# A two-layer cross-attention kernel: writes and loads of the stacked Q and K, their order on a queue, and two helpers' work moved between engines

## What is computed

```python
h = jnp.concatenate([x, latents], axis=1)             # 64 + 512 keys
q = (latents @ q_w + q_b).reshape(b, k_len, NH, DH)   # 512 queries
kv = (h @ kv_w + kv_b).reshape(b, p + k_len, NH, DH, 2)
attn = jnp.einsum('bkhd,bnhd->bhkn', q, kmat) / DH
attn = jax.nn.softmax(jnp.where(full_mask[:, None, None, :], attn, -jnp.inf), axis=-1)
attn_out = jnp.einsum('bhkn,bnhd->bkhd', attn, v).reshape(b, k_len, H)
attn_out = attn_out @ out_w + out_b + residual
out = gelu(rmsnorm(attn_out, postnorm_w) @ mlp_w1 + mlp_b1) @ mlp_w2 + mlp_b2
return out + residual
```

## Time and profile before

| | |
|---|---|
| median of three runs | 1864.66 us (1859.7 to 1866.77) |
| profiled execution, its own time | 1862.46 us |
| its span, first to last instruction | 1860.6 us |
| TensorE busy | 1642.2 us, 88% |
| VectorE busy | 1009.4 us, 54% |
| ScalarE busy | 703.4 us, 38% |
| GpSimd busy | 541.9 us, 29% |
| mean granted TensorE clock | 0.93 of 2.4 GHz |
| second attention, first scores to last | 766 to 1432 us |

### The profile page before, as it was taken

One profiled execution on the slowest core, in us unless ns is written; L12 is line 12 of the kernel. 1 busy time (PEld: TensorE's weight loads), 2 busy tenths in 40 slices (PEclk: granted clock), 3 DMA queues, 4 the chain that ended last, 5 costly groups with the idle time before them and its releaser, 6 DMA issues.

```text
span 1860.6 us, 23089 instructions
## 1 busy us (share of the span) xinstructions
PE 1642.2 (88%) x6993; PEld 1229.6 (66%) x6993; DVE 1009.4 (54%) x1612; ACT 703.4 (38%) x1260; POOL 541.9 (29%) x543
## 2 busy tenths in 40 slices
PE   5778887899999998888988898989886699999998
PEld 4667775667878786555665555655553477787886
DVE  3665565554333335667766766775787455334333
ACT  3433333431111111367556745663667232111111
POOL 2232245404040505133323422341358210404000
PEclk9788898999999998789988999998988799999999
DMA  5011023501010215223123223221221420101011
GB/s 176 1 40 63 23 91 100 177 1 46 0 45 0 91 70 186 68 83 112 61 72 94 87 61 109 65 91 61 95 84 46 151 81 1 46 0 45 0 41 50
DMA packets 60730, 126.13 MB, mean 68 GB/s; under 512 B 10397, under 2 KB 10722, under 8 KB 60642
## 3 DMA queue, kind: packets, MB, share of 16 engines
q1 hardware_dynamic: 53602, 102.08, 16.8%
q0 software_dynamic: 7040, 23.07, 4.1%
HBM read 90.25 MB, written 34.60 MB: 67 GB/s over the span
## 4 chain that ended last, share of the span: by engine, by line
PE 70%; DVE 14%; issue 6%; ACT 4%; DMA 3%; SPq 1%; POOL 0%; ACTq 0%; DVEq 0%; POOLq 0%
PE bank L2064 18%; PE bank L2052 17%; PE bank L1926 5%; DVE RA L1268 4%; PE bank L1961 3%; PE bank L1922 3%; PE bank L2023 3%; DVE FA L1501 3%; PE bank L1976 3%; PE bank L1977 2%; PE bank L1939 2%; PE bank L1748 2%; PE bank L1724 2%; PE bank L1943 2%; PE bank L1799 1%
## 5 line engine op out<-in xcount | busy, mean ns | idle before, releaser
L2064 PE MATMUL bank<-W,RA 128*128 128x512 f32 x1536 | 384.3, 402 | 25.3 <-DVE RA L1268 25.1
L2052 PE MATMUL bank<-RA,W 128*128 (+1 forms) x1536 | 374.7, 396 | 2.7 <-issue 2.3
L2064 PEld LDWEIGHTS bank<-W,RA 128*128 128x128 f32 x1536 | 290.3, 191 | 99.5 <-DVE RA L1268 31.2
L841 POOL TENSOR_TENSOR RA<-FA,RA 128x512 fp32r<-128x512 f32 (+1 forms) x160 | 216.0, 1354 | 423.9 <-ACT FA L1104 423.8
L2052 PEld LDWEIGHTS bank<-RA,W 128*128 128x128 f32 x1536 | 286.9, 188 | 74.9 <-issue 5.9
L1268 DVE TENSOR_TENSOR RA<-FA,RA 128x512 fp32r<-128x512 f32 (+2 forms) x308 | 274.7, 894 | 68.0 <-ACT FA L1104 54.5
L1160 ACT ACTIVATE FA<-bank,cols 128x512 f32<-128x512 f32 x128 | 88.2, 689 | 560.2 <-PE bank L2052 560.1
L1631 DVE CAST RA<-FA 128x512 fp32r<-128x512 f32 x128 | 62.5, 488 | 368.9 <-ACT FA L1160 368.7
L1103 ACT ACTIVATE RA<-bank 128x512 fp32r<-128x512 f32 (+1 forms) x320 | 192.4, 601 | 170.3 <-PE bank L1961 164.6
L1501 DVE TENSOR_REDUCE FA<-bank 128x1 f32<-128x512 f32 x256 | 169.1, 685 | 65.4 <-PE bank L1939 64.1
L1104 ACT ACTIVATE FA<-bank 128x512 f32<-128x512 f32 (+1 forms) x320 | 191.5, 599 | 0.0
(11 more groups left out here) (149 smaller groups left out, 1838.1 us busy)
## 6 DMA issues: line engine op xcount, KB each, us to landing
RA<-k_parts SPq DMA_DIRECT2D x96, 144.0 KB
FA<-after_layer SPq DMA_DIRECT2D x12, 1024.0 KB, 6.2
RA<-q_parts SPq DMA_DIRECT2D x96, 128.0 KB
k_parts<-FA SPq DMA_DIRECT2D x16, 576.0 KB, 3.2
after_att<-FA SPq DMA_DIRECT2D x32, 256.0 KB, 2.1
q_parts<-FA SPq DMA_DIRECT2D x16, 512.0 KB, 2.7
raw<-in_L_xattn_mlp_w_dram POOLq DMA_DIRECT2D x32, 256.0 KB, 3.4
RA<-after_att SPq DMA_DIRECT2D x12, 512.0 KB, 8.6
```

The costliest lines, as they stand in the source:

```text
L841: pool.tensor_tensor(pl[0:m, r, :], pf[0:m, r, :], ph[0:m, r, :].bitcast(F32), ALU.subtract).then_inc(p_lo_pool, 1)
L2052: op = pe.matmul(bank[FC1_BANK[i]][:, :], W[:, slot, a, k, i * P:(i + 1) * P], yT_[:, ds(b * (2 * KT * S) + (d * KT + k) * S, S)], start=( ...
L2064: op = pe.matmul(bank[4 + t][:, :], gs[:, a, i, t * P:(t + 1) * P], W[:, slot + 1, d, i, :], start=(i == 0 and a == 0 and d == 0), stop=(i ...
```

## The change

It does five things, all in the second attention.

1. `q_parts` and `k_parts` in DRAM hold, for each head, the three blocks of 32 rows in stacking order, one of them twice. `parts` issues three writes of [128 rows, 512 or 576] where there was one of [128, 2, 512 or 576].
2. `stack` loads 96 rows in one DMA for Q and one for K, where it took three each. Counts of the semaphores follow.
3. On SyncE's queue `pair(0)` stands behind `max_row`, and `pair(1)` behind sum row 2.
4. `lo_by_pool`: GpSimd makes the low parts of all four full tiles of a head and VectorE that of the context tile; before, GpSimd had two full tiles and every second context tile.
5. The copy of a head's result to `sg` is VectorE's, ahead of its sum in `o_sum`; ScalarE's `o_out` goes.

```diff
-    return t in (1, 3) or (t == TT and j % 2 == 0)
+    return t < TT
...
-STACK = 16 * 13
+STACK = 16 * 5
 def stack_count(c):
-    return 16 * 7 if c < 2 else STACK
+    return 16 * 3 if c < 2 else STACK
...
 def parts(x, nb, c):
...
-    sp.dma_start((q_parts, k_parts)[x][c % 2], (qt, kt)[x].bitcast(F32)).then_inc(parted[x][c % 2], 16)
+    to = (q_parts, k_parts)[x][c % 2]
+    for r, part in enumerate(((0, 0, 1), (0, 1, 0))[x]):
+        sp.dma_start(to[:, r, :, :], (qt, kt)[x][:, part, :].bitcast(F32)).then_inc(parted[x][c % 2], 16)
 def stack(nb, c, half):
...
-    for x, dst_, src_, order_ in ((0, QS, q_parts, (0, 0, 1)), (1, KS, k_parts, (0, 1, 0))):
-        wait_apart(sp, (parted[x][c % 2], at(0, nb, 32, 16 * (c // 2 + 1))))
-        rows_of = src_[c % 2].rearrange("(j p) h n -> p j h n", p=HD)
-        for r, part in enumerate(order_):
-            sp.dma_start(dst_[r * HD:(r + 1) * HD, c % 2, heads, :].bitcast(F32),
-                         rows_of[:, heads, part, :]).then_inc(to, 16)
+    for x, dst_, src_ in ((0, QS, q_parts), (1, KS, k_parts)):
+        wait_apart(sp, (parted[x][c % 2], at(0, nb, 96, 48 * (c // 2 + 1))))
+        sp.dma_start(dst_[0:3 * HD, c % 2, heads, :].bitcast(F32),
+                     src_[c % 2, heads].rearrange("j r p n -> (r p) j n")).then_inc(to, 16)
...
     if ahead:
         wait_apart(sp, (pb_free, at(0, b, USES, use1(f"{pre}KC{nc_}", last) + 1)))
         parts(1, nb, nc_)
-        pair(0)
     sums(HG * c + 1)
     if not (last and c == G - 1):
...
         max_row(b if c + 1 < G else b + 1, (c + 1) % G)
     if ahead:
+        pair(0)
+    sums(HG * c + 2)
+    if ahead:
         pair(1)
-    sums(HG * c + 2)
...
 def o_sum(h):
     j = h % HG
+    dve.wait_ge(pv_step, at(0, b, BSTEP, (h + 1) * (TT + 1)))
+    wait_apart(dve, (o_moved[h % 2], at(0, b, 128, 16 * (h // 2))))
+    dve.tensor_copy(sg[0:2 * HD + 1, h % 2, :], bank[6 + h % 2][0:2 * HD + 1, :]).then_inc(sg_ready, 1)
     dve.wait_ge(sg_ready, at(0, b, H, h + 1))
...
-parts = [nc.dram_tensor(n, (2, P, 2, m), F32, kind="Internal").ap() ...
+parts = [nc.dram_tensor(n, (2, HG, 3, HD, m), F32, kind="Internal").ap() ...
```

More of the change, by code:

```diff
@@ L335, in program @@
         pv_step = sem("pv_step")
+        o_free = sem("o_free")
         sg_ready = sem("sg_ready")
-        o_free = sem("o_free")
         o_moved = [sem("o_moved0"), sem("o_moved1")]
@@ L559, in sums @@
                         sp.wait_ge(sg_ready, at(0, b, H, h + 1))
-                        sp.dma_start(s16[h:h + 1, :], sg[2 * HD:2 * HD + 1, h % 2, :])\
-                            .then_inc(o_moved[h % 2], 16)
+                        sp.dma_start(s16[h:h + 1, :], sg[2 * HD:2 * HD + 1, h % 2, :]).then_inc(o_moved[h % 2], 16)
                     wait_apart(sp, (stored1, at(0, b, 16 * TT, 0)))
@@ L579, in batch @@
                             wait_apart(sp, (pb_full, at(0, b, USES, use1(f"R{G - 1}", last) + 1)),
-                                       (parted[0][1], at(0, b, 32, 32)), (parted[1][1], at(0, b, 32, 32)))
+                                       (parted[0][1], at(0, b, 96, 96)), (parted[1][1], at(0, b, 96, 96)))
                             for q in range(2):
@@ L1061, in hi @@
                             wait_apart(act, (parted["QK".index(kind[0])][(c + 1) % 2],
-                                             at(0, own, 32, 16 * ((c - 1) // 2 + 1) if c else 0)))
+                                             at(0, own, 96, 48 * ((c - 1) // 2 + 1) if c else 0)))
                     src = full(b, u, last, first)
@@ L1104, in exp @@
                         act.activation(pf[0:m, r, :], src, ACT.Exp, scale=SCALE1).then_inc(p_exp, 1)
[L1106 to L1110, removed]
                     for c in range(G):
@@ L1118, in batch @@
                                 hi(b, at_step[i], last)
-                            h, t = divmod(n - LAG - 1, TT + 1)
-                            if t == TT and h >= 0:
-                                o_out(h)
                             if last and c == G - 1 and i == OPEN_NORM + 3:
@@ L1129, in batch @@
                         hi(b, "nV1")
-                    o_out(H - 1)
                     if not last:
@@ L2139 @@
     out = nc.dram_tensor("out_0_dram", (B, S, D), F32, kind="ExternalOutput").ap()
-    parts = [nc.dram_tensor(n, (2, P, 2, m), F32, kind="Internal").ap() for n, m in (("q_parts", S), ("k_parts", NK))]
+    parts = [nc.dram_tensor(n, (2, HG, 3, HD, m), F32, kind="Internal").ap() for n, m in (("q_parts", S), ("k_parts", NK))]
     program(nc, *main, weights, *between, *parts, out)
```

## The result

The changed kernel takes 1963.74 us (median of four runs, 1962.92 to 1964.87) where before takes 1862.88: ratio 1.0541, 95% interval [1.0518, 1.0564], 101 us slower. Predicted were 1905 us and at most 1928. The sign was right, the size was not.

A forecast was written before the change was run, and what follows sets the result against it. TensorE, busy 88%, was taken as the bound, so only its waits and lower clock counted. Against 1862.5 us: queue +29.6 + 5.1, stack loads 0, start +16, relief -20, last batch +12 = +42.7, so 1905 us; range 1862 to 1928.

The forecast's parts named there:

- Four engines: Part writes to DRAM: 4 outer rows, so four of 16 engines carry each write, at 92 GB/s.
- A: The forecast itself: part writes on four engines; likeliest 1905 us, range 1880 to 1935, chance 0.78.
- B: Rival: part writes on 16 engines, k writes landing in 4.0 us; sum -33, 1830 us, range 1812 to 1852, chance 0.16.
- The three k writes land 1.6 + 9.6 = 11.2 us after the first issue: k_parts writes: 1.6 us fixed plus 9.6 us transfer on four engines; first score about 11.3 us after the first write.
- Nothing for the queue behind the fourth quarter: Ends of batches: no term; the queue was priced only where scores wait for the maxima row, +29.6 and +5.1 us.
- Lower clock: TensorE behind longer pauses: a longer stretch at the lower clock, +8 us, only in the high end of A's range.
- VectorE's relief, -20: TensorE's waits for VectorE, 31.1 us: two thirds taken back by moving low parts to GpSimd, -20 us, bounds -31 and -5.
- Start, +16: First two groups' writes: ScalarE waits for the first k write, V projections begin later; +16 us, low bound +1.
- Last batch, +12: Last batch on GpSimd, with extra low parts: third quarter +4, fourth +8, together +12 us, bounds +3 and +15.
- A's far end: High end of A's range: relief -8, late stacks +11, longer lower clock +8, +15 and others; +75 us, 1935.

The follow-up runs named there:

- e7: Kernel before with three part writes in a DRAM layout of 128 equally spaced rows outermost, and three loads per stack; 1876.5 us, ratio 1.0086.
- e14: Changed kernel with each narrow part write cut into four writes of one head; 1896.9 us, ratio 1.0202.
- e6: Kernel before with the new narrow part writes, but three loads of 32 rows per stack; 2014.4 us, ratio 1.0827.
- e17: Repeat of e15 for a profile: kernel before with new writes, merged stack loads and queue order; 1980.7 us, a single execution.
- e5: Changed kernel with the writes and stack loads of before; 1884.5 us, ratio 1.0116.
- e8: Changed kernel with the wide DRAM layout of e7 and three loads of 32 rows per stack; 1880.2 us, ratio 1.0092.
- e9: Kernel before with low parts on GpSimd and result copies on VectorE, writes and queue as before; 1887.8 us, ratio 1.0135.
- e15: Kernel before with new part writes, merged stack loads and queue order, without the low-part and copy changes; 1974.7 us, ratio 1.0616.
- e13: As e6, but two narrow writes, each block stored once, the loads taking one block twice; 1970.0 us, ratio 1.0586.

## Why the prediction was wrong

- *Four engines*: right (share 0.24 to 0.28, 91 to 99 GB/s; e7 and e14 by experiment). The narrow writes against wide ones are worth 84 us in the whole change; A minus B gave 75. That these two are close is luck: A was 59 us too low and B 50.
- *"The three k writes land 1.6 + 9.6 = 11.2 us after the first issue"*: the first step that failed. Measured were 12.9 (e6) and 13.2 to 13.7 (changed kernel, after the start). The rate was a little too low (2.9 us a write, not 3.2); the fixed part is 4.2 us, not 1.6. The 1.6 came from a write that sixteen engines share, and was carried over to one where each of four engines has four times the rows. So a first score came 13.7 to 14.1 us after the k write, not 11.3: 61.4 us for 34.7.
- *Nothing for the queue behind the fourth quarter*: the second, and it was no term at all. The prediction counted places where scores wait for the row, and priced the queue for these. Sum rows stand behind the same wait, and with edits 1 to 3 the reciprocal of a batch waits for them: the place is 22 us longer in e17, 15.7 of them this wait. In the changed kernel the wait is 3.4 us and the place still 15.0 longer; e5 and e8, with wide writes, are 15.5 and 17.2 longer there. So how the 15.0 divide between the queue and edits 4 and 5 stays open.
- *Lower clock*, only an end of A's range (+8), belongs in the sum: the first three steps of batch 1's third quarter take 5.6 us at a clock of 0.55 where they took 3.8 at 1.00. That the longer pause is the cause isn't shown. From the last score ahead of them to the first of them it is 5.8 us here; in e9, where that is 2.1 us, they take 5.6 us at 0.56, and in e17, where it is 3.6, they take 4.7 at 1.00.
- *VectorE's relief, -20*: in the trace it looks the wrong way round (+11.0). By experiment it isn't: edits 4 and 5 on top of the others are worth -11 (e15 to the changed kernel), recorded were -20 + 12 = -8. What the table sets against relief holds the price of edits 1 to 3 as well: from e17 to the changed kernel its two rows fall by 22.5 us. That the term came out right is luck, for it hides two errors: the copy in front of the join costs much more than 0.65 us a place (e9), and the narrow writes covered most of it.
- *Start, +16*: 17.5. *Last batch, +12*: 8.4, and 4.0 more after the attention.
- *A's far end*: its terms give +77, not +75. It would not have reached the measured 101 either.
- *Rival B* had the cause of its failure inside: it gave the queue order 36 us of gain, and alone the order costs 9, since the stack is as late as the row was early.

By medians: 112 measured for edits 1 to 3 where 51 was recorded, -11 for edits 4 and 5 where -8 was. So the error of 59 us is that of edits 1 to 3 (61). The trace of e17, itself 6 us longer than e15's median, puts 29 of it in the distances (64 for 35), 22 behind the fourth quarters, 11 between first scores and k writes, and 5 elsewhere.

What stays open: what fills the first 4 us of narrow writes; why the clock of e9 falls where TensorE is busy; how the changed kernel's 15.0 us behind fourth quarters divide; why the order alone spreads over 27 us from one execution to the next.

## What to carry to other kernels

In these runs a DMA's layout decided how many engines carry it: before a buffer's layout is changed for a better load, look at the outermost dimension of its write. A fixed cost read from a wide write (1.6 us) didn't hold for a narrow one (4.2). When a wait on a queue grows, follow every instruction behind it to its consumer, also those far from the place that the change is about. Two edits that would gain 12 us if they added up cost 26 together (e9), where the work of GpSimd and VectorE meets just ahead of a join; and a loss can lie hidden in a pause that another edit makes.

## What the runs showed of the hardware

- Writes of 128 rows with 4 outermost on their DRAM side run at 102 GB/s after 4.2 us (e13 and e6), so three of 288 KB are down 12.9 us after the first issue; with 128 or 32 equally spaced rows outermost the same bytes are down within 4.1 us (e7, three issues) or 7.7 (e14, twelve).
- A minimum of two 128x16 SBUF operands on VectorE takes 0.18 us (before, GpSimd idle), and 1.11 us (changed kernel) while GpSimd runs three low parts in a row (4.33 us). The Trainium skill (SBUF — State Buffer, who interferes with whom) says that such an instruction and one of GpSimd that reads SBUF exclude each other; these two rows agree.
- TensorE's granted clock was 0.50 for 17.1 us in e9, and TensorE was busy 16.3 of them; it had also been busy for the 2 us ahead of the fall.
